# First attention of a vision tower: heads laid out from SBUF to SBUF, the keys' transfers issued by SyncE's queue and the queries' by ScalarE's

## The reference, cut to what matters

```python
def reference(x, cls_tok, ...):                      # x: 32 samples, 64 x 256 x 4
    h = _L0_tok_ref(x, ...)                          # token mixer: exp(k), weighted sums over a local window, layer norm
    h = concatenate([cls_tok, h], axis=1)            # 257 rows of 256
    h = h + _L0_attn_ref(_layernorm(h), Wq, Wkv, Wout)
    h = h + _L0_ffn_ref(_layernorm(h), ...)          # second attention and 8 experts, 2 for each token
    return h

def _L0_attn_ref(tokens, Wq, Wkv, Wout):             # HEADS, DK, DV = 16, 16, 64
    q = split_heads(tokens @ Wq, HEADS)
    kv = split_heads(tokens @ Wkv, HEADS)
    k, v = kv[..., :DK], kv[..., DK:]
    q, k, v = l2norm(q), l2norm(k), l2norm(v)
    attn = square(relu(einsum('bhid,bhjd->bhij', q, k)))
    out = tanh_norm(einsum('bhij,bhjd->bhid', attn, v))
    return out.transpose(0, 2, 1, 3).reshape(b, n, h * d) @ Wout
```

## Time and profile before

| what | us |
|---|---|
| median of 3 runs | 3130.85 |
| lowest and highest run | 3129.27, 3133.87 |
| the profiled execution | 3139.85 |
| its span in the profile | 3138.1 |
| first attention, from the first product of sample 0 to the last | 101 to 1600 |

### The profile page before, as it was taken

One profiled execution on the slowest core, in us unless ns is written; L12 is line 12 of the kernel. 1 busy time (PEld: TensorE's weight loads), 2 busy tenths in 40 slices (PEclk: granted clock), 3 DMA queues, 4 the chain that ended last, 5 costly groups with the idle time before them and its releaser, 6 DMA issues. The chain is left out here.

```text
span 3138.1 us, 66657 instructions
## 1 busy us (share of the span) xinstructions
PE 2907.1 (93%) x21548; PEld 2217.3 (71%) x21549; DVE 2098.8 (67%) x5372; ACT 1442.7 (46%) x2948; POOL 1157.0 (37%) x966
## 2 busy tenths in 40 slices
PE   3899999999999999999966999999999972999998
PEld 1677777777777777777744666666766652999997
DVE  4577677677677777777734777777777855444444
ACT  0444544545545545445422555555555533444443
POOL 3324434434434334334321233333233324444443
PEclk7899999999999999999987999999999985999999
DMA  3424424424424424324302111111111101554544
GB/s 83 96 70 92 107 66 95 107 62 98 102 62 104 98 66 104 94 70 104 87 22 51 49 47 53 43 42 52 45 54 47 44 33 44 77 76 76 77 77 69
DMA packets 161126, 223.12 MB, mean 71 GB/s; under 512 B 30305, under 2 KB 125730, under 8 KB 161074
## 3 DMA queue, kind: packets, MB, share of 16 engines
q1 hardware_dynamic: 135138, 187.50, 23.9%
q0 software_dynamic: 25936, 34.95, 7.2%
HBM read 125.26 MB, written 97.08 MB: 71 GB/s over the span
## 5 line engine op out<-in xcount | busy, mean ns | idle before, releaser
L66 POOL TENSOR_TENSOR vrn<-vsm,inv_root 128x16 f32<-128x16 f32 x64 | 243.8, 3809 | 285.8 <-DVE vsm L836 285.8
L665 ACT ACTIVATE R<-psA 128x1024 f32<-128x1024 f32 x256 | 262.4, 1025 | 168.4 <-PE psA L1150 164.2
L857 DVE TENSOR_TENSOR PR<-R 128x1024 f32<-128x1024 f32 x256 | 321.3, 1255 | 0.0
L2512 POOL DMA_INDIRECT out_rows<-e_y,e_dest x137 | 213.7, 1560 | 289.8 <-DMA out_rows<-e_y,e_dest 182.2
L1904 DVE TENSOR_REDUCE m_nm<-psC 128x4 f32<-128x1028 f32 (+1 forms) x256 | 239.0, 956 | 72.0 <-PE psC L2177 71.4
L1165 PE MATMUL psA<-PR,V 128*64 128x258 f32 x2048 | 283.4, 398 | 0.0
L670 ACT ACTIVATE oTs<-psA 128x258 f32<-128x258 f32 x256 | 99.1, 387 | 358.1 <-PE psA L1165 352.3
L1783 ACT ACTIVATE m_PT<-psC 128x770 f32<-128x770 f32 x256 | 194.0, 810 | 137.3 <-PE psC L2205 137.3
L1210 PE MATMUL psA<-wout,OT 128*128 128x256 f32 x1024 | 244.6, 382 | 0.4 <-DVE OT L899 0.4
L1698 POOL DMA_INDIRECT xg<-tn,idx x124 | 124.5, 1004 | 318.6 <-DMA xg<-tn,idx 186.6
L1210 PEld LDWEIGHTS psA<-wout,OT 128*128 128x128 f32 x1024 | 188.7, 191 | 24.6 <-DVE OT L899 0.7
(11 more groups left out here) (417 smaller groups left out, 7633.0 us busy)
## 6 DMA issues: line engine op xcount, KB each, us to landing
ks<-kparts SPq DMA_DIRECT2D x256, 128.0 KB, 3.3
qs<-qparts SPq DMA_DIRECT2D x256, 128.0 KB, 3.8
e_x<-xg SPq DMA_DIRECT2D x143, 129.0 KB
xraw<-in_x SPq DMA_DIRECT2D x66, 256.0 KB
qparts<-qh SPq DMA_DIRECT2D x128, 128.0 KB, 2.4
kparts<-kh SPq DMA_DIRECT2D x64, 128.0 KB, 2.5
kparts<-kl SPq DMA_DIRECT2D x64, 128.0 KB, 2.4
qparts<-ql SPq DMA_DIRECT2D x64, 128.0 KB, 2.4
```

The costliest lines, as they stand in the source:

```text
L66: return pool.tensor_tensor(out, x, e.to_broadcast(list(out.shape)), ALU.pow)
L665: act.activation(R[:, p % 2].rearrange("p a t n -> p t a n"), ps[:, 0:2, :].rearrange("p t (a n) -> p t a n", a=2), ACT.Relu).then_inc(rel ...
L857: dve.tensor_tensor(PR[:, p % 2, :, :, 0:L], R[:, p % 2], R[:, p % 2], ALU.mult).then_inc(prob_done, 1)
L2512: pool.indirect_dma_start(out, bass.IndirectOffsetOnAxis(ap=dest[:, b % XD:b % XD + 1], axis=0), y[:, b % XD], None, compute_op=ALU.add).t ...
```

## The change

SP no longer stores to DRAM. For each half it issues eight DMAs from SBUF to SBUF: `kh` to the row offsets 0 and 32 of `ks`, `kl` to 16 and 48, each for the two row halves hh. It starts on `kh` when its squares are done (`k_sq`), on `kl` at `kl_done`; the second half waits for `sim_done` as before and now stands ahead of the load of x. ScalarE issues the queries' DMAs from its own stream: `first_queries` (8 DMAs) between `values(j, 0)` and R of pair 6, `second_queries` (8 DMAs, after `sim_done`) between R of pair 7 and `values(j, 2)`. Their landing is told by two new semaphores `q_moved0`, `q_moved1`, which TensorE's `sim` waits for beside `moved0`, `moved1`. ScalarE's `mixer(j)` now waits for all four, since DMAs read `kh` to `ql` until then. The scratch tensors go.

```diff
+        MOVES = 8 * 16
@@ block.sync
-            def keep_parts(tiles, rows, out): ...
-            def lay_out_keys(c, moved): ...
-            def lay_out_queries(c, moved): ...
+            def move_heads(to, part, at, moved):
                 for hh in range(2):
+                    sp.dma_start(to(64 * hh + at, hh), part[64 * hh:64 * hh + 64].bitcast(F32)).then_inc(moved, 16)
+
+            def move_keys(part, c, ats, moved):
+                for at in ats:
+                    move_heads(lambda row, hh: ks[row:row + 16, 4 * c:4 * c + 4].bitcast(F32), part[:, c], at, moved)
 
             def spread_heads(j, c):
-
+                moved = moved1 if c else moved0
+                if c == 0:
+                    sp.wait_ge(k_sq, j + 1)
+                else:
+                    need(sp, sim_done, PAIRS * j)
+                move_keys(kh, c, (0, 32), moved)
                 if c == 0:
                     sp.wait_ge(kl_done, j + 1)
-                    keep_parts((kh, kl), v.kparts, k_out)
-                    sp.wait_ge(ql_done, j + 1)
-                    keep_parts((qh, ql, qh), v.qparts, q_out)
-                    sp.wait_ge(k_out, 64 * j + 64)
-                    lay_out_keys(0, moved0)
-                    sp.wait_ge(q_out, 96 * j + 96)
-                    lay_out_queries(0, moved0)
-                else:
-                    need(sp, sim_done, PAIRS * j)
-                    lay_out_keys(1, moved1)
-                    lay_out_queries(1, moved1)
+                move_keys(kl, c, (16, 48), moved)
@@ loop of block.sync
                 spread_heads(now, 0)
+                spread_heads(now, 1)
                 sp.wait_ge(x2_ready, i + 3)
                 load_x(at)
-                spread_heads(now, 1)
@@ block.scalar
+            def move_queries(part, c, ats, moved):
+                for at in ats:
+                    for hh in range(2):
+                        to = 64 * hh + at
+                        act.dma_start(qs[to:to + 16, hh, 4 * c:4 * c + 4].bitcast(F32),
+                                      part[64 * hh:64 * hh + 64, c].bitcast(F32)).then_inc(moved, 16)
+
+            def first_queries(j):
+                act.wait_ge(q_sq, j + 1)
+                move_queries(qh, 0, (0, 48), q_moved0)
+                act.wait_ge(ql_done, j + 1)
+                move_queries(ql, 0, (16, 32), q_moved0)
+
+            def second_queries(j):
+                need(act, sim_done, PAIRS * j)
+                move_queries(qh, 1, (0, 48), q_moved1)
+                move_queries(ql, 1, (16, 32), q_moved1)
+
             def mixer(j):
                 act.wait_ge(q_done, j + 1)
+                need(act, moved0, MOVES * j)
+                need(act, moved1, MOVES * j)
+                need(act, q_moved0, MOVES * j)
+                need(act, q_moved1, MOVES * j)
@@ sample of block.scalar
                     values(j, 0)
+                    first_queries(j)
                 relu(i, 6)
                 if more:
                     values(j, 1)
                 take_outputs(i, d, 5)
                 relu(i, 7)
                 if more:
+                    second_queries(j)
                     values(j, 2)
@@ sim of block.tensor
-                    pe.wait_ge(moved0, 128 * i + 128)
+                    pe.wait_ge(moved0, MOVES * i + MOVES)
+                    pe.wait_ge(q_moved0, MOVES * i + MOVES)
```

More of the change, by code:

```diff
@@ L481, in store @@
                 sp.dma_start(a.hs[bass.ds(i, 1)].rearrange("n p m -> p (n m)"), h2[:]).then_inc(h2_stored, 16)
-            def keep_parts(tiles, rows, out):
-                for n, part in enumerate(tiles):
-                    for hh in range(2):
-                        sp.dma_start(rows[:, hh, n].rearrange("c x n -> x c n"),
-                                     part[64 * hh:64 * hh + 64].bitcast(F32)).then_inc(out, 16)
-            def lay_out_keys(c, moved):
-                for hh in range(2):
-                    for at in (0, 32):
-                        to = 64 * hh + at
-                        sp.dma_start(ks[to:to + 32, 4 * c:4 * c + 4].bitcast(F32).rearrange("p m n -> p (m n)"),
-                                     v.kparts[c, hh].rearrange("a (r m) n -> (a r) (m n)", m=4)).then_inc(moved, 16)
@@ L2738, in build @@
     v.last_fill = (nb + 1) % 2
-    v.kparts = nc.dram_tensor("kparts", (KT, 2, 2, P // 2, L), F32, kind="Internal").ap()
-    v.qparts = nc.dram_tensor("qparts", (KT, 2, 3, P // 2, L), F32, kind="Internal").ap()
     v.xg = nc.dram_tensor("xg", (NEXP * v.rows_e + v.idle_rows, ROW), F32, kind="Internal").ap()
```

17 lines of the change are left out of this document (6 added, 11 removed).

## The result

The changed kernel takes 3354.61 us (median of 4 runs, 3346.12 to 3356.17) beside 3130.47 us of the kernel before on the same chip (3129.27 to 3133.87). The ratio is 1.0709, its 95% interval 1.0689 to 1.0728: **224 us slower**. The forecast was 3280, its range 3180 to 3420. The profiled execution took 3356.17 us, with a span of 3354.5 us against 3138.1 before: 216.4 us more.

The account below looks back on a forecast made before the run. TensorE was taken to bound the first attention, 47.34 us a sample. A delay of 4.8 us over 31 samples (149), +2 for sample 0 and -3 of waits give +148 on 3130.85: about 3280 us, range 3180 to 3420.

Parts of the forecast that it names:

- The bound and the sign: First attention: TensorE sets the 47.34 us period, faster transfers give back at most 6.7 us; slower 0.85.
- The stall at `sim(i, 7)`: First eight ScalarE issues delay R of pair 6, so TensorE stands still for 8d - 1.6 = 2.8 us a sample.
- d: Spacing of ScalarE's DMA issues, taken as 0.55 us, with 0.47 and 0.66 as ends.
- The second lot and the chain: Sixteen issues make piece 3's squares, GpSimd's chain and `attend` 16d - 4.0 = 4.8 us late a sample, stall included.
- The front and the waits: Sample 0, prepared alone, costs net +2 us; later TensorE waits for transfers go, -3 us.
- +203: Whole-kernel cost in us if d is 0.66, at 6.6 us a sample.
- The likeliest case: ScalarE's issues held in order, d between 0.47 and 0.66: 3280 us, own range 3235 to 3335, chance 0.58.
- The queues hold each other up: SP and ScalarE issuing together lengthen issues: +363, 3490 us, in part 3330 to 3400; chance 0.18 shared with draining.
- The arithmetic drains before an issue: ScalarE's lots start later, 7.7 us a sample, +240, 3370 us; chance 0.18 shared with the queues' rival.
- The issues hide: Short issues fit ScalarE's gaps, below 0.20 to 0.25 us each; 3124 to 3129 us; chance 0.14.
- Transfers land late: TensorE or `mixer` waits for late transfers; 4 us of room for queries of pairs 0 to 3, no chance given.
- if the cover were gone, `mixer` would wait some tenths: SP's sixteen key transfers cost nothing; the second lot lands around 529 us, `mixer` needs it at 529.36 plus the delay.

Follow-up runs that it names:

- trial of forms: Ahead of the first attention of the changed kernel, SP and ScalarE issued five forms of SBUF-to-SBUF transfer, apart, then one form together; 3453.02 us, comparable with nothing.
- the spread version: Changed kernel with ScalarE's second lot issued one or two at a time where it idles, the rest by SP, waits split; 3134.79 us, ratio 1.0005.
- the last kernel: Changed kernel with all transfers issued by SP and waits placed on ScalarE where each memory is written again; 3130.26 us, ratio 0.9993.

## Where the prediction was right, and where not

**The bound and the sign** were right. ScalarE had half of its time free and yet only 0.9 us to spare at R of pair 6, and removing the path through DRAM had 6.7 us to give. The direct path alone took 5.3 us off TensorE's waits.

**The stall at `sim(i, 7)`** was right as a formula, 8d - 1.6. With the measured spacing of 0.66 it gives 3.68 us, and the trace has 3.69. Its input was mis-sized: d was taken as 0.55, and 0.66 is the upper end that the text kept. The step that failed here is "it has the source of the dearer and fewer pieces, so I take" the middle. The trial of forms shows that fewer pieces don't make an issue between SBUF tiles shorter; those of 16 pieces cost as much as those of 64. In a row of issues the price was 0.60 to 0.62 and the gap 0.04. The nearest row was `kparts<-kh`, also out of SBUF, at 0.628, and it should have been taken as it stood. Why transfers from DRAM of 4 KB rows were issued in 0.42 no run here tells.

**The second lot and the chain** were right in mechanism: started beside R of pair 7, ended before Vr of piece 2, GpSimd late at `attend`. By 16d - 4.0 and d = 0.66 a sample should lose 6.56 us, and it lost 6.94. The path is the one that the text walked: the squares came 7.06 us late in the sample shown, and `attend` followed them by the same 9.37 us as before. What the sum left out is TensorE at half clock. The text said that a fallen clock would add a cost; in the changed kernel it added little. Between `sim(i, 7)` and the next `sim(., 0)` TensorE waits for nothing and loses 2.88 us to the clock, but beside it the second lot delays the squares by 3.29 us, so the two don't add and only 0.59 us of waiting for `pcl` shows, at 0.41 us more than the idle time there before. What the clock adds is the later start of the second lot, some 0.5 us (R of pair 7 at 1.33 instead of 0.78 us behind `sim(i, 7)`). The forecast of "1 to 2 us" for the wait for `pcl` was too high for this reason. That the half clock fitted under the second lot's delay is luck: nothing in the prediction says so, and without the second lot it cost some 3 us a sample. That the two cover each other was shown from both sides: without the second lot the kernel gained 14 us, and with the first clock fall filled up it gained nothing.

**The front and the waits.** Net +2 was foretold for sample 0 at its `attend`; the first product came 1.7 us later and that `attend` 3.3 us later (109.98 against 106.66). The waits for transfers went, -3 as said.

**The sum by the same steps** with d = 0.66 was +203 in the text. Measured were +216 between the profiled spans and +224 between the medians, since the profiled execution of before was 9 us above its median and that of after was not. The likeliest case was thus 75 us short, 54 of them through d; the rest is the 0.4 us a sample above the formula (12 us, about the clock's part in the second lot's start) and those 9 us.

**The rivals.** *The queues hold each other up*: refuted. SP's issues of `ks` in the changed kernel have a median of 596 ns beside ScalarE's and 594 with all transfers on SP, and the trial gives 592 and 610 apart, 578 and 600 together. The Trainium skill ("Perfetto Trace Analysis", section "DMA Instruction — HWDGE (DVE, Sync)") draws a lock wait ahead of a descriptor generator that it says DVE and Sync share; between SP and ScalarE these rows show no such cost. What both queues at once did go with is later landing: from issue to landing the medians are 4.3 us for `kl`, 3.7 for `qh` and 4.6 for `ql` in the changed kernel, and 2.6 for each with all on SP. No engine waited for these transfers in the changed kernel. *The arithmetic drains before an issue*: refuted, the first issue starts 0.12 us after Vr does. *The issues hide*: false at 0.66, as its own condition said (0.20 to 0.25), but true for other places in the same stream: the spread version hides eight of them. The prediction asked how long an issue is and did not ask where else it could stand. *Transfers land late*: no chance was given, and in the changed kernel none was needed. The sentence "if the cover were gone, `mixer` would wait some tenths" holds for the keys of which it spoke: in the last kernel `mixer` waited for the high keys 3 times, 0.7 us at the longest, and once 1.6 us for the low ones. But the changed `mixer` waits for all four semaphores, the queries' too; with all transfers on SP it waited 5.41 us for the queries. That is a price of the change that the text didn't name and that doesn't show in the changed kernel.

The Trainium skill ("DMA: Bandwidth & Descriptors", section "Issuing engines are not separate DMA queues") says that several issuing engines save only the sequencer's issue time, usually small against the transfer. The first half agrees, splitting saved nothing here. For one transfer the second agrees as well, 0.62 us of issuing against 3.7 us to landing for `qh`. It doesn't help a row of them: the transfers overlap and the issues don't, and the eight of a lot hold ScalarE's order for 5.3 us.

## What to carry over

A DMA issue is an instruction in its engine's order, here 0.6 us long, and everything behind it comes later: count the issues in a row against the slack of the very next result that another engine waits for, not against the engine's busy share, and put them in ones and twos where the engine waits anyway. When TensorE is the bound, price a new wait as the wait plus the half clock that may follow it, unless something else is late by as much, and look at the granted clock of the stretch before explaining the rest. When transfers move to another queue, ask of every wait on them which memory it protects and when that is written again.

## What the hardware showed that was not expected

- Short waits of TensorE in an otherwise full stream were followed by half clock. After 3.69 us it was 6.8 us long in most samples, after 1.39 us 6.8 and in between 3.4, after 1.1 us 3.4 in about every fourth sample. With 6.8 us at half clock a sample was some 3 us longer where nothing else was late (the first lot alone), and only about 0.5 us longer where the second lot was late as well. Why waits of the same 1.1 us are followed by it in some samples and not in others stays open.
- Extra matmuls with an unused result made a kernel faster by 85 us (3340.11 to 3255.35), by keeping the clock.
- An issue between SBUF tiles had nearly the same price for 16, 64 and 128 pieces and for 64 and 128 KB, about 0.60 us in a row and 0.46 to 0.55 us as the first after a wait.
- With SP and ScalarE issuing at the same time the issues were as long as apart, but the transfers took 3.7 to 4.6 us to landing (`kh`, issued first, 2.6), against 2.6 with SP alone.
